# An earlier start, an added wait and one reordered maximum in the quantised block of a two-layer gated attention kernel

## What is computed

```python
x = x + tanh(g_xattn[0]) * attention0(layernorm(x), ctx)      # 16 heads of 8
x = x + tanh(g_ffn[0])   * quantised_ffn(layernorm(x))
x = x + tanh(g_xattn[1]) * attention1_causal(layernorm(x), ctx)
x = x + tanh(g_ffn[1])   * gated_scan(layernorm(x))
```

```python
def act_qdq(x):
    scale = max(max(abs(x)) / 32767, 1e-12)
    return clip(round(x / scale), -32768, 32767) * scale
x = act_qdq(x)
up   = act_qdq(x @ dequant4(w_up).T)
gate = act_qdq(x @ dequant4(w_gate).T)
sig  = fixed_u16(sigmoid(gate))
gate = act_qdq(gate * sig)
o    = act_qdq(gate * up)
return o @ dequant4(w_down).T
```

## Time and profile before

| | us |
|---|---|
| median of 3 runs | 343.93 |
| lowest, highest | 343.29, 344.03 |
| span of the profiled execution | 341.2 |
| DVE busy in it | 252.5 (74%) |
| PE busy | 279.0 (82%) |
| ACT busy | 192.6 (56%) |
| Pool busy | 136.7 (40%) |

### The profile page before, as it was taken

One profiled execution on the slowest core, in us unless ns is written; L12 is line 12 of the kernel. 1 busy time (PEld: TensorE's weight loads), 2 busy tenths in 40 slices (PEclk: granted clock), 3 DMA queues, 4 the chain that ended last, 5 costly groups with the idle time before them and its releaser, 6 DMA issues. The chain is left out here.

```text
span 341.2 us, 4468 instructions
## 1 busy us (share of the span) xinstructions
PE 279.0 (82%) x1424; PEld 160.7 (47%) x1424; DVE 252.5 (74%) x538; ACT 192.6 (56%) x303; POOL 136.7 (40%) x274
## 2 busy tenths in 40 slices
PE   0889899899989779985007888899998998999994
PEld 0558544455434345331005776664654654444462
DVE  5699875877996388889989977986596693441834
ACT  1673367556476746779589632446656446665232
POOL 6669893750050411870002059921386207131100
PEclk9999999999999999997556999999999999999998
DMA  7930100010000000000000002220001000000004
GB/s 204 336 146 3 69 32 10 27 73 10 1 8 3 0 0 2 1 0 0 1 0 0 2 0 92 94 100 2 10 25 76 8 0 10 1 0 3 0 1 123
DMA packets 9687, 12.55 MB, mean 37 GB/s; under 512 B 896, under 2 KB 5376, under 8 KB 9664
## 3 DMA queue, kind: packets, MB, share of 16 engines
q1 hardware_dynamic: 9232, 11.80, 9.7%
q10 hardware_dynamic: 432, 0.47, 0.7%
HBM read 4.27 MB, written 1.05 MB: 16 GB/s over the span
## 5 line engine op out<-in xcount | busy, mean ns | idle before, releaser
L1333 DVE TENSOR_REDUCE sb_nm<-ps_top 128x3 f32<-128x462 f32 (+2 forms) x168 | 96.0, 626 | 26.6 <-PE ps_top L953 13.9
L772 ACT ACTIVATE sb_pr<-ps_score 128x512 f32<-128x512 f32 (+1 forms) x148 | 82.3, 583 | 58.8 <-PE ps_score L985 49.2
L953 PE MATMUL ps_top<-sb_Kd,sb_Q 128*128 128x462 f32 (+3 forms) x240 | 69.7, 349 | 4.7 <-DVE sb_nm L1333 2.4
L985 PE MATMUL ps_score<-sb_Q,sb_Kd 128*128 128x512 f32 x119 | 54.4, 467 | 1.3 <-ACT sb_pr L772 1.0
L953 PEld LDWEIGHTS ps_top<-sb_Kd,sb_Q 128*128 128x128 f32 x240 | 42.6, 188 | 18.1 <-DVE sb_nm L1333 11.9
L626 POOL TENSOR_SCALAR sb_var<-sb_mv 128x4 f32<-128x4 f32 x16 | 4.7, 291 | 83.3 <-DVE sb_mv L1296 82.9
L985 PEld LDWEIGHTS ps_score<-sb_Q,sb_Kd 128*128 128x128 f32 x119 | 22.2, 188 | 31.6 <-ACT sb_pr L772 23.4
L1017 PE MATMUL ps_pv<-sb_pr,sb_V 128*32 128x512 f32 x256 | 34.1, 605 | 0.0
L620 POOL TENSOR_SCALAR_AFFINE_SELECT sb_pr<-sb_pr 128x512 f32<-128x512 f32 x16 | 10.6, 661 | 46.4 <-ACT sb_pr L772 46.4
L1353 DVE STREAM_TRANSPOSE sb_oq<-ps_pv 128x512 f32<-128x512 f32 x16 | 10.8, 700 | 12.4 <-PE ps_pv L1017 12.3
L643 POOL TENSOR_SCALAR sb_xn<-sb_xr,sb_nmean,sb_rstd 128x128 f32<-128x128 f32 x44 | 19.3, 453 | 1.2
(11 more groups left out here) (180 smaller groups left out, 556.5 us busy)
## 6 DMA issues: line engine op xcount, KB each, us to landing
sb_Q<-sb_qh SPq DMA_DIRECT2D x16, 256.0 KB, 2.3
sb_Q<-sb_ql SPq DMA_DIRECT2D x8, 256.0 KB, 3.3
sb_xr<-x SPq DMA_DIRECT2D x4, 256.0 KB, 7.7
out<-sb_xr SPq DMA_DIRECT2D x4, 256.0 KB, 2.5
sb_wsb<-w SPq DMA_DIRECT2D x1, 704.0 KB, 9.0
sb_wf<-wffn SPq DMA_DIRECT2D x1, 576.0 KB, 8.6
sb_wkr<-wkr SPq DMA_DIRECT2D x2, 256.0 KB, 7.1
sb_Q<-sb_nmT SPq DMA_DIRECT2D x16, 32.0 KB
```

Source lines behind the costliest of these rows:

```text
L772: act.activation(pr[:, k % PRING, q0:T], score_bank(B * layer + b, t)[:, q0:T], ACT.Exp, scale=SCALE).then_inc(exp_r, 1)
L953: ins = pe.matmul(cols[:, c0:c1, :], Q4[n % 3][:, g, P * qt:P * qt + P], Kd[n % 3][:, g, j:j + c1 - c0, 0:keys], start=True, stop=not mask ...
L985: ins = pe.matmul(ps[:, :], Kd[n % 3][:, g, j, 0:P], Q4[n % 3][:, g, :], start=True, stop=True, skip_group_check=True)
L1333: dve.tensor_reduce(nm[:, :, :].rearrange("p t h -> p (t h)")[:, f0:f0 + heads], top[k % MRING][:, 0:keys * heads].rearrange("p (h k) -> p ...
```

## The change

Three edits. PE's wait ahead of `keep_warm(6)` is for the first `outer` instead of the second. Pool's clearing of `Q4[1]` waits for the third `last16` as well. DVE takes the maximum of the first up tile, `absmax(12)`, ahead of `whole_top(1)` and the first rounding of the gate, and no longer behind it.

```diff
@@ def clear_early():
                 pool.wait_ge(fmm, 24)
                 pool.wait_ge(o_r, B)
+                pool.wait_ge(n3_r, 3)
                 pool.memset(Q4[1][:, :, :].bitcast(F32), 0.0).then_inc(q4_clear, 1)
@@ tensor queue
                     for k in range(2, 4):
                         global_top(k)
                     pe.wait_ge(fev, 24)
-                    pe.wait_ge(o_r, 2)
+                    pe.wait_ge(o_r, 1)
                     keep_warm(6)
                     global_top(4)
                     keep_warm(2)
@@ def ffn():
                 for t in range(12):
                     absmax(t)
                 part_max(1, 12)
+                absmax(12)
                 whole_top(1)
                 scale_of(1)
                 gate16(0)
-                absmax(12)
                 gate16(1)
                 gate16(2)
                 absmax(13)
```

## The result

| | before | after |
|---|---|---|
| median, us | 343.73 (4 executions, 343.29 to 344.03) | 341.55 (4 executions, 341.40 to 341.67) |
| span of the profiled execution, us | 341.2 | 339.7 |

The ratio of the two is 0.9942, with a 95% interval of 0.9928 to 0.9956: by the ratio 2.0 us faster (the medians differ by 2.2), where 1.6 was forecast. The span came out at 339.7 us against a forecast of 339.6. So what has to be explained is not the block, but the way from a span to a time.

The account below looks back on a forecast made before the run. It took a DVE chain before the down projections as the bound, the fourth maximum delayed by PE's fill and Pool's clearing; 1.60 + 0 + 0 - 0 = 1.6 us off 343.93 gave 342.3 us, range 341.8 to 343.6.

Parts of the forecast that it names:

- The sum: Whole change: 1.60 + 0 + 0 - 0 = 1.6 us saved, span to 339.6, median 343.93 to 342.3.
- the six: Unread PE matmuls of `keep_warm(6)` ahead of `global_top(4)`: start at 179.38, end at 184.4 to 184.6; alone worth nothing.
- the covers: Between `part_max(4)` and `whole_top(4)`: PE's fill and DVE's held `product16(1)`; earlier fill alone 0, later clearing 0.62, both 1.60 us.
- Rival 1: PE's clock falls in the gap behind the earlier fill, slowing `keep_warm(4)` and `down(0)`: 1.5 us net loss, 345.4; 5%.
- Rival 2: Pool's clearing collides in its new place, holding the fourth `last16` for 0.57 us: net saving 1.03, 342.9; 10%.
- Rival 3: `product16(1)` was slow beside ACT and PE, not Pool, and stays at 2.65 us: nothing moves, 343.9; 3%.

Follow-up runs that it names:

- the second comparison: The changed kernel run again, 6 executions beside 23 of the kernel before: 342.05 us against 343.38, ratio 0.9960.
- the run with the clearing at the wrong place: Changed kernel, but Pool's clearing waits for the first `last16` (n3_r 1), beside the scaling for `down(0)`: 344.71 us, ratio 1.0029.

## Why the prediction was wrong

**The sum was right.** Step by step: the six were forecast to start at 179.38, 0.15 us behind the read, and did so by the changed kernel's own clock (179.52 behind 179.37). `product16(1)` fell to 1.01 (forecast 1.02). `whole_top(4)` came 1.65 us nearer to the maximum (1.60 forecast, bounds 1.5 to 1.63, so 0.02 beyond them). ACT was free 0.47 us before `product(1)` was released (0.5). The clearing stood beside the residual at no cost (0). The moved maximum cost 0.00 and its gain became idle time (0), though 1.35 us of it and not 0.6: the prediction had left out that the roundings behind it were 0.75 us longer beside Pool. The ranking of the covers held too: alone the earlier fill gave 0.0 us, the later clearing 0.8 (0.62), together 1.4 by that run's median and 1.65 by its rows.

**The step that failed** is in the paragraph headed "Sum": "I take the saving off the median". It takes the median of three executions, 343.93, as the time that goes with the profiled span of 341.2. I had seen that the three times lay 2.1 to 2.8 us above that span and treated the spread as something that lies around the span. It is not: the difference is 1.97 us within 0.07 in all 147 executions, and the spans themselves vary. A span of 341.2 stands for an execution of 343.2, and 339.6 + 1.97 = 341.6 would have been within 0.1 of the result. The median of three that I used was 0.5 us above the 343.39 that 78 executions gave, and 0.7 above the 343.2 that goes with the profiled span. The lower end of the range, 341.8, hung on the same base, and fell with it. The width above (to 343.6) was spent on rivals; none was kept for a base that is too high.

**What chance adds.** The four executions of after in the result held none of the tail and the four of before held two of it, so the first ratio shows 2.0 us; the second comparison shows 1.4, and all of them together 1.67. The median of the second comparison, 342.05, would have lain within the range. That the first lay below it is the base that was too high and the luck of four executions together; with the pooled 341.72 the miss is 0.1 us.

**The rivals.** Rival 1 did not occur: PE's gap was 0.57 us and the granted clock was 1.00 from 184 us on, through `down(0)`. Its gap was worked out wrongly: 12 records at the rate of `keep_warm(4)`, 8 in 1.99 us, are 3.0 us and not 2.6, which leaves a gap of 2.1 and not 2.5. Its mechanism is real, by the run with the clearing at the wrong place, and the net time of 345.4 was near that run's 344.71, for which it shares the blame with a held scaling. Rival 2 did not occur: the clearing began 0.23 us behind the residual and was not queued behind it. The run beside the third `last16` speaks against its mechanism, at least where the `last16` begins first. The rule of the Trainium skill, "SBUF — State Buffer", section "Who interferes with whom", that an instruction with two SBUF inputs contends only with a GpSimd instruction that reads, agrees with the 1.81 us of the clearing there; the 1.67 us of L627, which reads, agree as well (the median of this line's 16 runs in the kernel before is 0.20 us). The page's other sentence, that whichever issues first holds the port, does not agree with the recorded starts: VectorE's instruction began first, by 0.04 us and by 0.12 us, and was held both times to 0.81 us behind the end of the clearing. Whether a recorded start is the moment of which the page speaks, no run here shows. Rival 3 is refuted by the 1.01 us.

## What to carry to other kernels

Take a saving that is read from a profile off the time of the profiled execution, that is its span plus the constant that lies around it (1.97 us in this program), and not off a median of three; here the fastest of the three, 343.29, was nearer to that time than the middle one. When two covers end at nearly the same place on one path, price each alone and the pair: by their rows they were worth 0, 0.75 and 1.65 us here. In these runs a clearing on Pool was free beside instructions of VectorE with two SBUF inputs (1.79 to 1.82 us) or a PSUM input (0.74 to 0.75 us); beside a rounding or a scaling it cost 1.6 to 1.7 of its 1.8 us, even when it was released just behind it.

## What was not expected of the hardware

An instruction of VectorE that had been started 0.12 us before Pool's clearing was held for 1.71 us, to 0.81 us behind the clearing's end, as if it had hardly begun. And after a PE idle time of 4.88 us, with the product at the lower clock, the twelve records that followed it without a gap had the clock up for most of `down(0)`, where eight records behind a gap of 1.08 us had not. Moving one maximum of 0.6 us took 0.75 us off roundings that it does not touch.
